# Twelve-sublayer decoder: a new order of the matmuls in the large experts, one indirect weight load per quad in the small experts

## Chip, cores and metric

One core of one Trainium2 chip runs the whole program. The metric is the device time of one execution in microseconds, as the median of several runs. Less is better.

## What is computed

The input `x` is 128 sequences of 64 tokens with 128 features (8192 tokens). Twelve sublayers follow one another, each `x = layernorm(x + f(x))`. They are attentions, feed-forward layers and mixtures of experts. The change touches three of them, the mixtures in which tokens are sorted by expert:

```python
# L0_attn ("moe_first"): 8 experts, top 2 of a softmax, 128 -> 512 -> 128, gelu
hid = gelu(x @ w1[e] + b1[e]); out = hid @ w2[e] + b2[e]; y = sum over the 2 chosen e of topw * out
# L1_ffn ("L_ffn" in the profile): 32 experts, top 1, 128 -> 32 -> 128, relu twice
h = relu(x @ w1[e] + b1[e]); y = relu(h @ w2[e] + b2[e])
# L3_ffn ("moe_last"): 8 experts, top 1 with a capacity, 128 -> 512 -> 128, gelu
```

All numbers are float32.

## The kernel before

Each of the three mixtures works in the same way. A router (matmuls and many small VectorE steps, `choose` and `plan`) gives every token a row, a "slot", in a buffer in HBM in which the tokens of one expert are contiguous. POOL scatters the token rows there (`slot_x`) with indirect DMAs, 128 rows each. The experts then run over tiles of slots, and POOL gathers the results back from `slot_y` with indirect DMAs, after which the residual sum and the layer norm are made. The tokens are cut into parts (16, 32 and 16 token tiles in the large mixtures, two halves in the small one), so that the scatters of the next part and the gathers of the part before are issued by POOL while the tiles of the present part run. POOL waits for counts of finished tiles (`out_done`) before some of its scatters, which spreads them over the tiles.

Large experts, `moe` (L665): `J` tiles of 256 slots, 85 in moe_first and 53 in moe_last. Every tile loads the packed weights of its expert (`load_expert` L970, 578 KB, one plain DMA from SP into one of `RING` = 4 buffers) and its rows (`load_slots` L981, 128 KB, one of `XRING` = 3). TensorE works in the order that the loop at L1074 to L1078 spells out: `hidden(j)` (L1048, the first matmuls, 4 of 256 columns into two PSUM banks), `turn(j + 1)` (L1039, two transposes of the next tile's rows), `output(j)` (L1059, the second matmuls, 8 of 128 columns, which need the gelu of tile j). The profile shows each float32 matmul as two instructions, so a tile has 8 at L1055 and 16 at L1066. ScalarE makes four gelus of a tile (L1113) and the copy of the next transposed rows (L1104). VectorE evicts the output with its bias (`evict` L931, L936). SP's queue runs, per tile, `load_slots(j + 3)`, `load_expert(j + 3)`, `store_slots(j)`; the store waits for the eviction of tile j, so the row load that stands behind it in the queue is issued after that eviction. There is one PSUM bank for transposes, and two for the hidden values, so `hidden(j + 1)` also waits for the gelus of tile j (L1051).

Small experts, `moe_small` (L2570): 32 "quads" of four slot tiles of 128, each slot tile with its own expert. `load_expert` (L2737) reads the expert's number into a register, then loads its first weights (16 KB, L2745) and its second ones with the biases (`down`, 32 KB, L2747); it runs four times per quad, for g = 0 and 2 on SP and for 1 and 3 on ScalarE's queue, three quads ahead. TensorE's order (L2853 to L2859) is already `turn(j + 2)`, `hidden(j + 1)`, `output(j)`. POOL's program (L2897 to L2925) issues the 32 scatters of part 0, then those of part 1, spread by waits for `out_done`, and then chunk after chunk four gathers and two small steps of the layer norm.

## Time and profile before

| | us |
|---|---|
| Median of 3 runs | 3681.12 (3676.68 to 3685.07) |
| The profiled execution, its own time | 3685.81 |
| Its span | 3684.1 |
| moe_first, first to last eviction of a tile | 103.0 to 579.1 (85 tiles) |
| Small experts, first to last eviction of a quad | 1708.1 to 1864.1 (32 quads) |
| moe_last, first to last eviction of a tile | 3397.5 to 3642.8 (53 tiles) |

PE is TensorE, DVE VectorE, ACT ScalarE, POOL GpSimd, SP SyncE; a "q" behind an engine's name is its queue of DMA issues and register work. In a timeline a row is a run of equal instructions, with its start, its duration from first start to last end, and in brackets how long the engine sat idle before it and what ended that. "remote" is an end of waiting that the profile can't put to a recorded instruction. PEclk is the granted clock of TensorE, 1.00 being 2.4 GHz and 0.50 being 1.2 GHz. A row by stretch has the stretch, its length, the busy time and number (x) of the instructions asked for, PEclk, the share of the DMA engines' time and GB/s.

### The profile page before, as it was taken

What the parts mean: (1) busy time and instruction counts of PE and PEld (TensorE: products, weight loads), DVE (VectorE), ACT (ScalarE), POOL (GpSimd) and SP (SyncE); (2) the same over time, 40 slices, a digit from 0 to 9 for tenths busy, and PEclk for the clock granted to TensorE, in tenths of its full rate; (3) what the DMA queues carried; (4) which work ended last, traced back from release to release, by engine and by line L of the source; (5) the groups of instructions that cost most, each with busy time, mean ns of one, the idle gap of its engine ahead of it and who ended that gap; (6) DMA issues with size and microseconds to landing.
All of it is one profiled execution on the core that took longest, in us unless ns stands there. A gap on an engine that the chain in (4) does not pass through costs nothing. (4 is left out here: it accounts for less than half of the span.)

```text
span 3684.1 us, 83888 instructions
## 1 busy us (share of the span) xinstructions
PE 2954.5 (80%) x28814; PEld 2049.7 (56%) x28814; DVE 2179.3 (59%) x5986; ACT 1819.7 (49%) x3516; POOL 1824.6 (50%) x1735
## 2 busy tenths in 40 slices
PE   2778877897888789953529997996999869995895
PEld 2667765674555556642316665664444536664784
DVE  2111134656888568862347886777898678884124
ACT  0333334744555456621216665775466676661342
POOL 3542254535777655526365554664033655553335
PEclk9988988899999799975559998998999889996997
DMA  8655652020101021214621112221000012222674
GB/s 283 185 168 177 187 163 86 24 8 25 41 35 45 38 72 69 71 45 119 171 59 43 58 54 88 83 89 54 1 1 1 2 29 64 73 66 87 198 218 145
DMA packets 325160, 315.45 MB, mean 86 GB/s; under 512 B 111348, under 2 KB 244885, under 8 KB 324504
## 3 DMA queue, kind: packets, MB, share of 16 engines
q1 hardware_dynamic: 283240, 261.98, 23.3%
q0 software_dynamic: 16384, 33.59, 3.0%
q10 hardware_dynamic: 25264, 16.40, 1.5%
q8 instruction: 154, 2.52, 0.3%
q14 instruction: 118, 0.97, 0.1%
HBM read 167.28 MB, written 60.69 MB: 62 GB/s over the span
## 5 line engine op out<-in xcount | busy, mean ns | idle before, releaser
L1066 PE MATMUL moe_first_out_ps<-moe_first_expert_w,moe_first_hid 128*128 128x128 f32 x1360 | 214.2, 310 | 92.5 <-ACT moe_first_hid L1113 55.1
L1113 ACT ACTIVATE moe_first_hid<-moe_first_hid_ps,moe_first_expert_w 128x256 f32<-128x256 f32 x340 | 139.2, 471 | 268.4 <-PE moe_first_hid_ps L1055 150.7
L936 DVE TENSOR_TENSOR moe_first_tile_y<-moe_first_out_ps,moe_first_expert_w 128x256 f32<-128x256 f32 x85 | 36.1, 425 | 379.2 <-PE moe_first_out_ps L1066 221.8
L1066 PEld LDWEIGHTS moe_first_out_ps<-moe_first_expert_w,moe_first_hid 128*128 128x128 f32 x1360 | 191.0, 211 | 110.3 <-DVE moe_first_tile_y L936 47.0
L1132 POOL DMA_INDIRECT slot_x<-x_tok,moe_first_slots x128 | 123.8, 968 | 109.6 <-DVE moe_first_slots L908 48.6
L1055 PE MATMUL moe_first_hid_ps<-moe_first_tile_xT,moe_first_expert_w 128*128 128x256 f32 x680 | 173.1, 400 | 3.1 <-issue 2.6
L794 POOL DMA_INDIRECT moe_first_token_y<-slot_y,moe_first_slots x128 | 123.8, 968 | 94.9 <-issue 66.7
L1865 POOL TENSOR_TENSOR causal_k_blocks<-causal_k_T,headmask 128x1024 f32<-128x1024 f32 x64 | 121.3, 1897 | 99.5 <-PE causal_scores L1475 94.0
L1865 POOL TENSOR_TENSOR alibi_k_blocks<-alibi_k_T,headmask 128x1024 f32<-128x1024 f32 x64 | 121.2, 1896 | 94.1 <-PE alibi_scores L1475 90.1
L1865 POOL TENSOR_TENSOR full_k_blocks<-full_k_T,headmask 128x1024 f32<-128x1024 f32 x64 | 120.7, 1896 | 84.2 <-PE full_scores L1475 79.2
L1113 ACT ACTIVATE moe_last_hid<-moe_last_hid_ps,moe_last_expert_w 128x256 f32<-128x256 f32 x212 | 86.6, 471 | 140.8 <-PE moe_last_hid_ps L1055 122.5
L3154 PE MATMUL L_ffn_experts<-weights_odd,x_T 128*128 128x512 f32 x256 | 146.5, 655 | 1.3 <-ACT L_ffn_expert_out L3250 1.3
L1865 POOL TENSOR_TENSOR keys_k_blocks<-keys_k_T,headmask 128x1024 f32<-128x1024 f32 x64 | 120.9, 1899 | 45.7 <-PE keys_scores L1475 42.1
L1055 PEld LDWEIGHTS moe_first_hid_ps<-moe_first_tile_xT,moe_first_expert_w 128*128 128x128 f32 x680 | 131.9, 205 | 20.6 <-issue 4.4
L1066 PE MATMUL moe_last_out_ps<-moe_last_expert_w,moe_last_hid 128*128 128x128 f32 x848 | 125.0, 295 | 21.6 <-issue 11.7
L3079 DVE SCALAR_TENSOR_TENSOR L_ffn_combined<-L_ffn_expert_out,L_ffn_mix,L_ffn_combined 128x128 f32<-128x128 f32 x448 | 128.7, 350 | 3.9
L1066 PEld LDWEIGHTS moe_last_out_ps<-moe_last_expert_w,moe_last_hid 128*128 128x128 f32 x848 | 110.5, 195 | 32.8 <-issue 16.0
L1865 POOL TENSOR_TENSOR diff_k_blocks<-diff_k_T,headmask 128x1024 f32<-128x1024 f32 x64 | 121.7, 1912 | 10.8 <-POOL diff_k_T L1852 5.9
L3315 POOL TENSOR_SCALAR L_ffn_ms_eps<-L_ffn_ms 128x4 f32<-128x4 f32 x16 | 3.7, 231 | 239.6 <-DVE L_ffn_ms L3087 239.4
L936 DVE TENSOR_TENSOR moe_last_tile_y<-moe_last_out_ps,moe_last_expert_w 128x256 f32<-128x256 f32 x53 | 22.4, 423 | 167.7 <-PE moe_last_out_ps L1066 125.5
L1722 DVE TENSOR_REDUCE keys_maxima<-keys_scores 128x8 f32<-128x512 f32 x128 | 87.7, 685 | 49.7 <-PE keys_scores L1475 48.7
L1619 ACT ACTIVATE diff_probs_T<-diff_pT 128x512 f32<-128x512 f32 x128 | 76.1, 595 | 79.5 <-PE diff_pT L1489 79.2
(561 smaller groups left out, 8941.3 us busy)
## 6 DMA issues: line engine op xcount, KB each, us to landing
moe_first_expert_w<-in_L_attn_experts SPq DMA_DIRECT2D x85, 578.0 KB
moe_last_expert_w<-in_L_ffn_experts SPq DMA_DIRECT2D x53, 578.0 KB
moe_first_tile_x<-slot_x SPq DMA_DIRECT2D x85, 128.0 KB
slot_y<-moe_first_tile_y SPq DMA_DIRECT2D x85, 128.0 KB
slot_x<-blank ACTq DMA_DIRECT2D x2, 4992.0 KB
L_ffn_tile_x<-slot_x SPq DMA_DIRECT2D x32, 256.0 KB
slot_y<-L_ffn_tile_y SPq DMA_DIRECT2D x32, 256.0 KB
moe_last_tile_x<-slot_x SPq DMA_DIRECT2D x53, 128.0 KB
```

The lines of the kernel that those rows point to most:

```text
L794: pool.indirect_dma_start(y_in[:, p, k, r, :], None, slot_y[part][0:NTS[part] * SLOT_TILE, :], bass.IndirectOffsetOnAxis(slots[:, part, r, ...
L936: dve.tensor_tensor(y_out[:, q, :, :], out_bank[q][:, 0:SLOT_TILE].rearrange("p (s d) -> p s d", s=SPAN), over(wall[:, j % RING, 2 * FF + ...
L1055: last = pe.matmul(hid_bank[h][:, SLOT_TILE * (b % 2):SLOT_TILE * (b % 2) + SLOT_TILE], wall[:, j % RING, 128 * b:128 * b + 128], xT[:, j ...
L1066: last = pe.matmul(out_bank[j % 2][:, D * s:D * s + D], hid[:, j % 2, b, TILE * s:TILE * s + TILE], wall[:, j % RING, FF + D * b:FF + D * ...
L1113: act.activation(hid[:, j % 2, b, :], hid_bank[b // 2][:, SLOT_TILE * (b % 2):SLOT_TILE * (b % 2) + SLOT_TILE], gelu, bias=wall[:, j % RIN ...
L1132: pool.indirect_dma_start(slot_x[part][:, :], bass.IndirectOffsetOnAxis(slots[:, part, r, t:t + 1], 0), net.x_tok[:, origin[part] + t, :], ...
L1619: act.activation(probs_T[:, t.p, 4 * g:4 * g + 4, :].rearrange("p k t -> p (k t)"), pT_bank[:, :], ACT.Copy)\
L1722: dve.tensor_reduce(maxima[:, t.p, heads], src, AX_X, ALU.max).then_inc(max_done, 1)
L1865: pool.tensor_tensor(k_blocks[:, t.p, :, :], keys.to_broadcast([128, 8, TILE]), lanes.to_broadcast([128, 8, TILE]), ALU.mult).then_inc(spr ...
L3079: last = dve.scalar_tensor_tensor(combined[:, p, k, :], expert_out[:, p, k, e, :], w, combined[:, p, k, :], ALU.mult, ALU.add)
L3154: pe.matmul(expert_bank[g][:, :], net.x_T[:, TILE * t:TILE * t + TILE], experts_s[:, 4 * g:4 * g + 4, :].rearrange("p e d -> p (e d)"), st ...
L3315: pool.tensor_scalar(ms_eps[:, :], ms[:, :], 1.0 / D, 1e-6, ALU.mult, ALU.add).then_inc(ms_eps_done, 1)
```

## The change

Large experts: TensorE's loop is now `turn(j + 2)`, `hidden(j + 1)`, `output(j)`, with `turn(0)`, `turn(1)` and `hidden(0)` ahead of it; ScalarE copies `copy_turned(j + 2)` after the gelus of tile j. The weight ring has five buffers, and SP loads weights four tiles ahead. The ring of rows still has three, loaded three tiles ahead.

Small experts: the four `down` loads of a quad from SP and ScalarE are replaced by one indirect DMA on POOL, which fetches 128 rows of 1028 bytes, 32 for each of the four experts. The row numbers are made by VectorE: five small steps once (`lane`), and six in each `plan`. POOL's program is one loop over the quads now: in step j the scatters of part 1 that are due, a chunk's gathers where one is due, `load_down(j + 3)`, and a layer norm step where one is due. TensorE waits for the two kinds of weights by two semaphores.

```diff
-    RING, XRING = 4, 3
+    RING, XRING = 5, 3
...
-                for j in range(3):
+                for j in range(4):
                     load_expert(j)
...
                     if j + 3 < J:
                         load_slots(j + 3)
-                        load_expert(j + 3)
+                    if j + 4 < J:
+                        load_expert(j + 4)
                     store_slots(j)
...
                 turn(0)
+                turn(1)
+                hidden(0)
                 for j in range(J):
-                    hidden(j)
+                    if j + 2 < J:
+                        turn(j + 2)
                     if j + 1 < J:
-                        turn(j + 1)
+                        hidden(j + 1)
                     output(j)
...
                 copy_turned(0)
+                copy_turned(1)
...
-                    if j + 1 < J:
-                        copy_turned(j + 1)
+                    if j + 2 < J:
+                        copy_turned(j + 2)
...
+                    for g in range(4):
+                        own = slice(H * g, H * g + H)
+                        last = dve.tensor_scalar(row_f[own, :], expert_f[own, :].rearrange("p (n g) -> p g n", g=4)[:, g, :],
+                                                 float(E - 1), float(H), ALU.min, ALU.mult)
+                    step(last)
+                    step(dve.tensor_tensor(row_at[:, :], row_f[:, :], lane[:, 0:1].to_broadcast([128, J]), ALU.add))
+                    dve.tensor_copy(down_at[:, part, :], row_at[:, :]).then_inc(planned, 1)
...
-                eng.dma_start(down[H * g:H * g + H, j % RING, :], w_down[bass.ds(e, 1), :, :].rearrange("o p w -> p (o w)"))\
...
-                    pe.wait_ge(w_landed[j % RING], 128 * (j // RING + 1))
+                    pe.wait_ge(w_landed[j % RING], 64 * (j // RING + 1))
+                    pe.wait_ge(d_landed[j % RING], 16 * (j // RING + 1))
...
+                def load_down(j):
+                    part, n = divmod(j, J)
+                    if j >= RING:
+                        pool.wait_ge(out_ready, j - RING + 1)
+                    if n == 0:
+                        pool.wait_ge(planned, 3 * part + 3)
+                    pool.indirect_dma_start(down[:, j % RING, :], None, rows,
+                                            bass.IndirectOffsetOnAxis(down_at[:, part, n:n + 1], 0)).then_inc(d_landed[j % RING], 16)
...
+                pool.wait_ge(planned, 1)
+                for t in range(K):
+                    scatter(0, t)
+                for j in range(3):
+                    load_down(j)
+                pool.wait_ge(planned, 4)
+                due = {}
+                for t in range(K):
+                    due.setdefault(1 + t * (J - 6) // K, []).append(t)
+                gather_at = {q - 2: c for q, c in after_quad.items()}
+                for j in range(ALL):
+                    if j in due:
+                        pool.wait_ge(out_done, j)
+                        for t in due[j]:
+                            scatter(1, t)
+                    if j in gather_at:
+                        gather(gather_at[j])
+                    if j + 3 < ALL:
+                        load_down(j + 3)
+                    if j - 1 in after_quad:
+                        tail.inverse_std(pool, after_quad[j - 1])
```

## Rows read from the trace of the kernel before

**Rows 1.** The page: share of TensorE, and the second matmuls of moe_first.
```profile
PE 2954.5 (80%) x28814; PEld 2049.7 (56%) x28814; DVE 2179.3 (59%) x5986; ACT 1819.7 (49%) x3516; POOL 1824.6 (50%) x1735
...
L1066 PE MATMUL moe_first_out_ps<-moe_first_expert_w,moe_first_hid 128*128 128x128 f32 x1360 | 214.2, 310 | 92.5 <-ACT moe_first_hid L1113 55.1
```

**Rows 2.** By stretch: busy us and number (x) of the evictions at L936.
```profile
195.00:223.00 28.00, 3.40 (x8) 1.00 0.75 223
223.00:286.00 63.00, 2.97 (x7) 0.76 0.46 136
...
3529.00:3575.00 46.00, 4.87 (x12) 1.00 0.77 232
```

**Rows 3.** Timeline (start, duration, engine, line, operation, count): TensorE over one steady tile.
```profile
337.08 1.89 PE L1055 MATMUL moe_first_hid_ps<-moe_first_tile_xT,moe_first_expert_w 128*128 128x256 f32 x8
...
339.03 1.36 PE L1066 MATMUL moe_first_out_ps<-moe_first_expert_w,moe_first_hid 128*128 128x128 f32 x8
...
340.23 1.06 PE L1066 MATMUL moe_first_out_ps<-moe_first_expert_w,moe_first_hid 128*128 128x128 f32 x8
...
341.12 1.89 PE L1055 MATMUL moe_first_hid_ps<-moe_first_tile_xT,moe_first_expert_w 128*128 128x256 f32 x8
```

**Rows 4.** Timeline: the eviction of the tile before, and the next row load.
```profile
337.28 0.42 DVE L936 TENSOR_TENSOR moe_first_tile_y<-moe_first_out_ps,moe_first_expert_w 128x256 f32<-128x256 f32 x1 [3.61 <-PE moe_first_out_ps L1066]
...
338.14 0.47 SPq L987 DMA_DIRECT2D moe_first_tile_x<-slot_x  x1
```

**Rows 5.** DMA issues: KB each, median us from issue to landing.
```profile
diff_xT_in<-x_T SPq DMA_DIRECT2D x16, 256.0 KB, 2.3
...
keys_x_in<-x_tok SPq DMA_DIRECT2D x16, 256.0 KB, 3.6
```

**Rows 6.** Timeline: moe_first while POOL issues sixteen indirect DMAs without a pause.
```profile
304.07 1.20 POOL L1132 DMA_INDIRECT slot_x<-x_tok,moe_first_slots  x1 [0.20 <-issue]
...
308.69 2.25 PE L1066 MATMUL moe_first_out_ps<-moe_first_expert_w,moe_first_hid 128*128 128x128 f32 x16
...
315.60 0.42 DVE L936 TENSOR_TENSOR moe_first_tile_y<-moe_first_out_ps,moe_first_expert_w 128x256 f32<-128x256 f32 x1 [8.66 <-remote]
...
323.19 0.94 POOL L794 DMA_INDIRECT moe_first_token_y<-slot_y,moe_first_slots  x1 [0.30 <-issue]
...
328.30 0.42 DVE L936 TENSOR_TENSOR moe_first_tile_y<-moe_first_out_ps,moe_first_expert_w 128x256 f32<-128x256 f32 x1 [12.27 <-PE moe_first_out_ps L1066]
```

**Rows 7.** By stretch: busy us and number of the evictions at L2708, small experts.
```profile
1708.00:1762.00 54.00, 7.61 (x11) 0.53 0.63 170
1762.00:1787.00 25.00, 4.16 (x6) 0.50 0.65 166
1787.00:1866.00 79.00, 10.27 (x15) 0.54 0.58 148
```

**Rows 8.** Timeline, SP's queue: a quad of the small experts, no indirect DMA.
```profile
1762.23 0.43 SPq L2767 DMA_DIRECT2D slot_y<-L_ffn_tile_y  x1
...
1765.53 0.34 SPq L2745 DMA_DIRECT2D L_ffn_expert_up<-in_L_ffn_up  x1
1766.08 0.33 SPq L2747 DMA_DIRECT2D L_ffn_expert_down<-in_L_ffn_down  x1
1766.46 0.43 SPq L2767 DMA_DIRECT2D slot_y<-L_ffn_tile_y  x1
```

**Rows 9.** Timeline of POOL and VectorE: small experts, three scatters to a quad.
```profile
1754.06 0.96 POOL L2905 DMA_INDIRECT slot_x<-x_tok,L_ffn_slots  x1 [0.30 <-issue]
...
1755.96 0.69 DVE L2708 COPY L_ffn_tile_y<-L_ffn_out_ps 128x512 f32<-128x512 f32 x1 [4.69 <-remote]
...
1756.92 0.96 POOL L2905 DMA_INDIRECT slot_x<-x_tok,L_ffn_slots  x1 [1.90 <-DVE L_ffn_tile_y L2708]
```

**Rows 10.** Timeline of POOL and VectorE: small experts, the first eight gathers.
```profile
1787.79 0.98 POOL L2917 DMA_INDIRECT L_ffn_token_y<-slot_y,L_ffn_slots  x1 [27.39 <-DMA slot_y<-L_ffn_tile_y]
...
1796.40 0.69 DVE L2708 COPY L_ffn_tile_y<-L_ffn_out_ps 128x512 f32<-128x512 f32 x1 [9.84 <-remote]
```

More of the change, by code:

```diff
@@ L2612, in moe_small @@
         expert_f, expert_of = sb("expert_f", [128, NT]), sb("expert_of", [128, PARTS, NT], I32)
+        below, lane_i, lane_of, lane = sb("below", [128, 1]), sb("lane_i", [128, 1], I32), sb("lane_of", [128, 1], I32), sb("lane", [128, 1])
+        row_f, row_at, down_at = sb("row_f", [128, J]), sb("row_at", [128, J]), sb("down_at", [128, PARTS, J], U32)
         up = sb("expert_up", [128, RING, 4, H])
@@ L2632, in moe_small @@
         scattered = [sem(f"rows_scattered{n}") for n in range(PARTS)]
-        w_landed = [sem(f"expert_landed{n}") for n in range(RING)]
+        w_landed = [sem(f"expert_up_landed{n}") for n in range(RING)]
+        d_landed = [sem(f"expert_down_landed{n}") for n in range(RING)]
         x_landed = [sem(f"slot_x_landed{n}") for n in range(XRING)]
@@ L2721, in _ @@
                 dve.wait_ge(fixed, 1)
+                step(dve.tensor_reduce(below[:, :], before[:, :], AX_X, ALU.add))
+                step(dve.tensor_scalar(lane_i[:, :], below[:, :], -1.0, None, ALU.add))
+                step(dve.tensor_scalar(lane_of[:, :], lane_i[:, :], H - 1, None, ALU.bitwise_and))
+                step(dve.tensor_copy(below[:, :], lane_of[:, :]))
+                step(dve.tensor_scalar(lane[:, :], below[:, :], -1.0, float(H - 1), ALU.mult, ALU.add))
                 for part in range(PARTS):
@@ L2742, in load_expert @@
                 if n == 0:
[L2743 removed]
+                    eng.wait_ge(planned, 3 * part + 2)
                 e = eng.value_load(expert_of[0:1, part, at:at + 1], min_val=0, max_val=E - 1)
                 eng.dma_start(up[:, j % RING, g, :], w_up[bass.ds(e, 1), :, :].rearrange("o p h -> p (o h)"))\
[L2746 to L2747 removed]
                     .then_inc(w_landed[j % RING], 16)
@@ L2899, in _, with scatter @@
                     pool.wait_ge(net.cleared[1 + n], 16)
-                for part in range(PARTS):
-                    pool.wait_ge(planned, 2 * part + 1)
-                    for t in range(K):
-                        if part and t:
-                            pool.wait_ge(out_done, J * (part - 1) + 1 + t * (J - 6) // K)
-                        pool.indirect_dma_start(slot_x[part][:, :], bass.IndirectOffsetOnAxis(slots[:, part, t:t + 1], 0),
-                                                net.x_tok[:, part * K + t, :], None).then_inc(scattered[part], 16)
+                def scatter(part, t):
+                    pool.indirect_dma_start(slot_x[part][:, :], bass.IndirectOffsetOnAxis(slots[:, part, t:t + 1], 0),
+                                            net.x_tok[:, part * K + t, :], None).then_inc(scattered[part], 16)
+                rows = w_down.rearrange("e p w -> (e p) w")
+                def load_down(j):
[6 more added lines that the diff above has]
+                                            bass.IndirectOffsetOnAxis(down_at[:, part, n:n + 1], 0)).then_inc(d_landed[j % RING], 16)
                 def gather(c):
@@ L2918, in gather @@
                                                 bass.IndirectOffsetOnAxis(slots[:, part, t:t + 1], 0)).then_inc(gathered[p], 16)
-                for c in range(CHUNKS):
-                    if c % PC == 0:
+                pool.wait_ge(planned, 1)
[19 more added lines that the diff above has]
+                        tail.inverse_std(pool, after_quad[j - 1])
+                for c in late:
+                    if c == late[0]:
                         gather(c)
-                    if (c + 1) % PC:
+                    if c + 1 < CHUNKS:
                         gather(c + 1)
```

2 lines of the change are left out of this document (removed).

## Prediction

> **What bounds the kernel now.** I read the page first: TensorE is busy for 80% of the span and no other engine for more than 59% [rows 1]. Only the three mixtures are touched, and they fill about 877 us between first and last eviction (476, 156 and 245 us in the table), so next I read how fast their tiles follow one another. In moe_first one tile follows another after 4.04 us where nothing disturbs (341.12 - 337.08) [rows 3], but 84 intervals take 476.1 us, 5.67 each, so 137 us go to something else. In moe_last 52 intervals take 245.3 us, 4.72 each, and 35 us are lost. The view by stretch shows where: 8 evictions fall into one stretch of 28 us, 7 into the next of 63 us [rows 2].
>
> In the steady tile TensorE has no gap, yet it isn't at its own pace. Its second matmuls come in two halves of eight. The last eight take 0.89 us (340.23 to 341.12), the first eight 1.20 us (339.03 to 340.23), for the same work [rows 3]. The first eight each need a gelu that ScalarE is only just making; the page lists that releaser for this line [rows 1]. That wait of 0.31 us per tile is what the new order can remove. The first matmuls and the two transposes fill the rest, 337.08 to 339.03.
>
> In the lost time nobody works: the second matmuls of a tile start at 308.69 and last 2.25 us, so they end at 310.94, but the eviction that needs them starts at 315.60 after 8.66 us of idle, ended "remote", and the one after it at 328.30. Through this stretch POOL issues sixteen indirect DMAs, 1.27 us apart (19.1 us over 15 intervals) [rows 6]. In the timeline every such stall of several us lies within a run of indirect DMAs and ends soon after it. I conclude that signals between engines pass badly while POOL issues them. This decides how I price the second half of the change, which gives POOL more of them.
>
> **Large experts: second matmuls one tile later.** In the steady tile the gelus of tile j now finish under output(j - 1), turn(j + 2) and the start of hidden(j + 1). The period becomes 4.04 - 0.31 = 3.73 us. Eight stretches with no run of indirect DMAs, or a short one, hold 51 evictions (the first and the last of them in rows 2), so up to 51 x 0.31 = 16 us.
>
> What is late next is the row load. turn(m) now stands straight behind output(m - 3); before, a whole tile's work more lay ahead of it. The load of rows m still leaves SP's queue behind the store of tile m - 4, that is after its eviction. From the end of output(m - 4) (337.08) to that issue (338.14) it is 1.06 us [rows 3, 4]. No row gives this load's own time to landing; loads of 256 KB take 2.3 to 3.6 us [rows 5]. From the landing to the end of output(m - 2) it is one full period, 3.73. Two periods are thus at least 1.06 + L + 3.73. With L = 2.3 this is 3.55 us per tile and doesn't bind; from L = 2.7 it binds; at L = 3.3 all the gain is gone; with L = 3.6 it is 4.20 us per tile, worse than now. A 128 KB load with little in front of it is nearest to 2.3, but DMA share is already 0.75 and 0.77 in such stretches [rows 2], so I let a tail of late loads take 0.1 us per tile: 51 x 0.2 = -10 us. turn is in order on TensorE, and hidden and output are queued behind it, so a late load costs its full lateness.
>
> In the disturbed tiles the order has a second effect. When signals stop, TensorE can run on through what is already released. Before, that ended at the second matmuls of the current tile, at most; now hidden(j + 1) and output(j) are both released by gelus of tile j, so up to hidden's and turn's 1.95 us (337.08 to 339.03) [rows 3] more gets done. But where this has used up the loaded rows, the restart waits for a store and a load (1.06 + 2.3 us), and the gain is gone. I count half of the 1.95 us, some 0.9 us at each restart. There are 24 runs of indirect DMAs behind the first scatter stretches of the two mixtures, like that in rows 6: -22 us. In the first scatter stretches themselves POOL sets the pace (64 scatters at 1.26 us are 81 us of 90), and I take 0. The fifth weight buffer and the load four tiles ahead keep the old lead in time: the wait for out_done before load_expert(j + 4) is the same as that before load_expert(j + 3) with four buffers. It costs and brings nothing, since the weights aren't what a steady tile waits for. Sum for the large experts: -32 us. Ends: -68 (0.31 on all 138 tiles and 25 on restarts) and +22 (138 x 0.16, rows always late).
>
> **Small experts: down weights from POOL.** Three stretches [rows 7].
>
> While part 1 is scattered, 11 evictions take 54 us. A run of three scatters ends at 1755.02, the eviction comes 0.94 us behind it, and POOL resumes 0.96 us after that [rows 9]. So a quad is the run (3.5 us) plus 1.9 us, 5.4 us, and this is what the stretch shows. One more indirect DMA makes the run 1.26 us longer, in ten quads: +12 us. Ends 0 (signals pass between the DMAs) and +13.
>
> Between scatters and gathers SP's queue sets the pace: store to store is 4.23 us without a gap. A down load costs from the end of the up issue (1765.87) to its own end (1766.41), 0.54 us, twice per quad on SP [rows 8]. Without both a quad could take 3.15 us. A lone indirect DMA now falls into each, so I take 0.6 us off in 6 quads: -4 us. Ends -6 and +7 (6 x 1.26).
>
> While gathers run, 15 quads take 79 us. Eight gathers in a row held one eviction back from the end of its matmuls to 1796.40, 9.84 us of idle [rows 10]. Here 13 loads come between 32 gathers; about 8 of them lengthen a run by 1.26 us: +10 us. Ends -13 (SP's relief of about 0.85 us counts in all 15 quads) and +16. load_down(j + 3) also queues behind four gathers (5 us) and their wait for stored tiles, and hidden(j + 3) waits for it; three quads of lead, 8 us and more, hide that.
>
> At the start four load_downs come behind the 32 scatters and before the first turns are signalled: +2 us, ends 0 and +5. The added VectorE steps (5 once, 6 in each plan, small) lie under the scatters of part 0, 32 x 1.26 = 40 us; uncovered they would be about 4 us. Sum: 12 - 4 + 10 + 2 = +20 us, ends -19 and +41.
>
> The Trainium skill, DMA: Bandwidth & Descriptors, section Rules for kernel authors, says to coalesce small transfers, as below 64 KB one pays mostly overhead; its section Anatomy of one DMA gives 2.0 us fixed for each DMA issued from GpSimd. By it four loads of 32 KB in one are a plain gain. The rows above agree only where SP's queue sets the pace [rows 8]; where POOL's runs do, the count on POOL is what costs [rows 9]. What that rule would make of the time is the first rival.
>
> **The sum.** -32 + 20 = -12 us. Against the profiled execution's own time, 3685.8, this is 3673.8; it lay 4.7 us above the median of the runs, so for the median 3681.1 - 12 = 3669 us.
>
> **Rivals.**
>
> First, the relief of the queues counts more than the runs on POOL: the small experts follow SP at about 0.5 us less per quad, 32 x 0.5 = -16 us, with -32 in the large ones: -48, 3633 us. For it: SP's queue is full in rows 8 and signals do pass at times within a run. Against: in two of three stretches the evictions follow the ends of the runs.
>
> Second, and slower: the rows land late. If a row load takes 3.6 us in most steady tiles, these cost 51 x 0.16 = +8 us, and every restart waits for rows, so nothing is gained there. With +20 in the small experts this is +28, 3709 us. It decides from L = 3.3 us on. For it: rows 5's upper end, and the shorter period makes the queues fuller. Against: the lower end, and that SP issues the rows right behind the store.
>
> Third, the two halves cancel: the restarts bring nothing beyond -10 to -20 and the small experts lose as much: about 3681 us. TensorE then waits for the same runs on POOL in another order.
>
> **How the numbers follow.** Forecast 0.42, first rival 0.20, second 0.22, third 0.16. A difference under 0.2% (7.4 us) can't be told from no change here. Faster by more: 0.20 from the first rival and 0.34 of the forecast, 0.54. Within: 0.08 of the forecast and 0.12 of the third, 0.20. Slower: 0.22 and 0.04, 0.26. The range reaches to both outer rivals, 3633 to 3706.
>
> **What would show it.** Steady tiles of moe_first every 3.7 to 3.8 us with both halves of L1066 equal (0.89 us); if they are 4.0 or more and TensorE's idle before L1044 is ended by the row load, the second rival is right. In the small experts 1.26 us more from eviction to eviction while part 1 is scattered; if they stay at 5.4 or fall, the first rival is. The prediction is wrong if the stalls aren't tied to POOL's runs, or if a load by row numbers costs POOL another time than a gather.

## The result, and the profile after

| | before, us | after, us |
|---|---|---|
| Median of 4 runs each, in turn on one chip | 3678.9 (3670.8 to 3685.1) | 3712.6 (3707.6 to 3715.8) |
| Span of the profiled execution | 3684.1 | 3713.8 |
| moe_first, first to last eviction | 476.1 | 465.6 |
| Small experts, first to last eviction | 156.0 | 183.7 |
| moe_last, first to last eviction | 245.2 | 246.4 |

The changed kernel takes 1.0089 times as long, 95% interval 1.0069 to 1.0109: 34 us more, where 12 us less was forecast. The stages say where. The small experts cost 28 us more (20 was forecast), and the large ones give back 9 us in sum instead of 32. A stretch that nobody touched, from the last eviction of the small experts to the first of moe_last, takes 1533.5 us before and 1540.8 after, and 1535.9 to 1541.8 us in the runs below with times like these. moe_first, with its stalls, varies by more: the new one takes 465.6 us here, and 475.6 and 458.8 us in two runs below. So I read single stages with care. One of the six executions of `small`, below, took 6130.7 us, and its ratio leaves that one out.

First the steady tile, in the timeline of the changed kernel: TensorE, VectorE's evictions, and SP's row load (start, duration, engine, line, operation).

```profile
378.94 0.42 DVE L936 TENSOR_TENSOR moe_first_tile_y<-moe_first_out_ps,moe_first_expert_w 128x256 f32<-128x256 f32 x1 [3.31 <-PE moe_first_out_ps L1067]
378.95 1.89 PE L1056 MATMUL moe_first_hid_ps<-moe_first_tile_xT,moe_first_expert_w 128*128 128x256 f32 x8
...
379.39 0.36 SPq L993 DMA_DIRECT2D slot_y<-moe_first_tile_y  x1
379.79 0.47 SPq L987 DMA_DIRECT2D moe_first_tile_x<-slot_x  x1
...
380.68 1.95 PE L1067 MATMUL moe_first_out_ps<-moe_first_expert_w,moe_first_hid 128*128 128x128 f32 x16
...
382.67 0.42 DVE L936 TENSOR_TENSOR moe_first_tile_y<-moe_first_out_ps,moe_first_expert_w 128x256 f32<-128x256 f32 x1 [3.31 <-PE moe_first_out_ps L1067]
...
383.20 0.44 PE L1045 MATMUL moe_first_turn_ps<-ident,moe_first_tile_x 128*128 128x128 f32 x2 [0.57 <-DMA moe_first_tile_x<-slot_x]
```

The sixteen second matmuls are one unbroken run now, where rows 3 had two uneven halves, and from eviction to eviction the tile takes 3.73 us (378.94 to 382.67), as worked out. But the transposes behind them wait: the load of the rows was issued at 379.79, and they were used at 383.20, 3.41 us later. The table of waits (engine and line, what it waited for: us in total, times, longest) has this for the whole of both mixtures:

```profile
PE moe_first_turn_ps L1045 <- DMA moe_first_tile_x<-slot_x: 46.5, 20, 8.3
PE moe_last_turn_ps L1045 <- DMA moe_last_tile_x<-slot_x: 32.8, 19, 3.8
PE moe_first_hid_ps L1056 <- ACT moe_first_hid L1118: 25.6, 13, 5.3
```

79 us of waiting for rows is what the second rival described. They are of two sorts. Each of these 39 waits can be paired with the eviction four tiles earlier, behind whose store the row load stands in SP's queue. For 12 of them (14 us) that eviction came at once behind its matmuls, and the load was slow, as above: 3.7 us from issue to use (median). For the other 27 (65 us) that eviction was itself held back, by 0.5 to 14 us, and the load was then as quick as the lower bound, 2.5 us (median). One of these 27:

```profile
353.37 1.95 PE L1067 MATMUL moe_first_out_ps<-moe_first_expert_w,moe_first_hid 128*128 128x128 f32 x16
...
357.10 1.95 PE L1067 MATMUL moe_first_out_ps<-moe_first_expert_w,moe_first_hid 128*128 128x128 f32 x16
358.99 0.76 DVE L936 TENSOR_TENSOR moe_first_tile_y<-moe_first_out_ps,moe_first_expert_w 128x256 f32<-128x256 f32 x2 [8.90 <-remote]
...
359.85 0.47 SPq L987 DMA_DIRECT2D moe_first_tile_x<-slot_x  x1
...
362.10 0.44 PE L1045 MATMUL moe_first_turn_ps<-ident,moe_first_tile_x 128*128 128x128 f32 x2 [3.05 <-DMA moe_first_tile_x<-slot_x]
```

The row of 358.99 holds two evictions at once: the first had been due behind the matmuls of 353.37, which end at 355.32. Only after it could the load be issued, and TensorE, which had run on meanwhile, waited 3.05 us for it. The third line of the table I had not expected at all: TensorE waits for ScalarE's gelus, the very wait that the new order was to remove, 13 times, 2 us on average.

The stretches of rows 2, by evictions again:

```profile
195.00:223.00 28.00, 2.55 (x6) 0.94 0.72 215
223.00:286.00 63.00, 3.99 (x10) 0.84 0.56 166
```

16 tiles pass in these 91 us, 15 before. The second stretch has 10 instead of 7, the first 6 instead of 8.

In the small experts POOL's run between two evictions is longer, as in this timeline of POOL and VectorE, which answers to rows 9:

```profile
1742.15 0.97 POOL L2920 DMA_INDIRECT slot_x<-x_tok,L_ffn_slots  x1 [2.71 <-DVE L_ffn_tile_y L2723]
1743.47 0.69 DVE L2723 COPY L_ffn_tile_y<-L_ffn_out_ps 128x512 f32<-128x512 f32 x1 [1.59 <-PE L_ffn_out_ps L2863]
...
1745.95 0.98 POOL L2931 DMA_INDIRECT L_ffn_expert_down<-in_L_ffn_down,L_ffn_down_at  x1 [0.30 <-issue]
1747.23 0.97 POOL L2920 DMA_INDIRECT slot_x<-x_tok,L_ffn_slots  x1 [0.30 <-issue]
...
1751.03 0.98 POOL L2931 DMA_INDIRECT L_ffn_expert_down<-in_L_ffn_down,L_ffn_down_at  x1 [0.31 <-issue]
...
1753.60 0.69 DVE L2723 COPY L_ffn_tile_y<-L_ffn_out_ps 128x512 f32<-128x512 f32 x1 [9.44 <-DMA moe_first_token_y<-slot_y,moe_first_slots]
...
1755.90 0.69 DVE L2723 COPY L_ffn_tile_y<-L_ffn_out_ps 128x512 f32<-128x512 f32 x1 [1.61 <-PE L_ffn_out_ps L2863]
```

Two quads' DMAs, eight in all, run without a pause from 1742.15 to 1752.01. One eviction still comes at their start (1743.47), the next only 1.59 us after their end, and then two come 2.3 us apart. (The gather of moe_first that the row of 1753.60 names as the end of VectorE's wait was done long before; what ended the wait isn't recorded.) Two quads in 12.4 us are 6.2 each, where rows 9 gave 5.4. Cut at the 12th and the 17th eviction, whose start times the timeline has, the small experts read:

| us between evictions | 1 to 12 (scatters) | 12 to 17 (quiet) | 17 to 32 (gathers) |
|---|---|---|---|
| before | 56.3 | 21.4 | 78.2 |
| after | 67.1 | 18.0 | 98.6 |

### The profile page after: what moved, and what is told of

Read it like the earlier page. It is cut to its first block and busy times, and to the rows that moved or that the text cites. A ratio compares the mean times of both kernels' runs of the same rounds, so it can differ in the third digit from the quotient of the medians.

```text
span 3713.8 us, 83586 instructions
## 1 busy us (share of the span) xinstructions
PE 2932.1 (79%) x28814; PEld 2039.1 (55%) x28814; DVE 2182.6 (59%) x6003; ACT 1829.6 (49%) x3516; POOL 1856.1 (50%) x1767
## 5 line engine op out<-in xcount | busy, mean ns | idle before, releaser
L936 DVE TENSOR_TENSOR moe_first_tile_y<-moe_first_out_ps,moe_first_expert_w 128x256 f32<-128x256 f32 x85 | 35.7, 423 | 373.2 <-PE moe_first_out_ps L1067 188.3
L1056 PE MATMUL moe_first_hid_ps<-moe_first_tile_xT,moe_first_expert_w 128*128 128x256 f32 x680 | 187.2, 423 | 41.7 <-ACT moe_first_hid L1118 25.6
L1067 PEld LDWEIGHTS moe_first_out_ps<-moe_first_expert_w,moe_first_hid 128*128 128x128 f32 x1360 | 177.9, 203 | 16.5 <-issue 9.9
L1067 PE MATMUL moe_first_out_ps<-moe_first_expert_w,moe_first_hid 128*128 128x128 f32 x1360 | 178.1, 285 | 9.7 <-issue 8.4
L1870 POOL TENSOR_TENSOR diff_k_blocks<-diff_k_T,headmask 128x1024 f32<-128x1024 f32 x64 | 121.7, 1913 | 10.9 <-POOL diff_k_T L1857 5.9
L936 DVE TENSOR_TENSOR moe_last_tile_y<-moe_last_out_ps,moe_last_expert_w 128x256 f32<-128x256 f32 x53 | 22.4, 424 | 177.7 <-PE moe_last_out_ps L1067 108.1
L1108 ACT ACTIVATE moe_first_tile_xT<-moe_first_turn_ps 128x256 f32<-128x256 f32 x85 | 32.9, 387 | 167.1 <-PE moe_first_turn_ps L1045 79.2
L1727 DVE TENSOR_REDUCE full_maxima<-full_scores 128x8 f32<-128x512 f32 x128 | 87.8, 686 | 45.8 <-PE full_scores L1480 44.8
L1727 DVE TENSOR_REDUCE causal_maxima<-causal_scores 128x8 f32<-128x512 f32 x128 | 87.8, 686 | 45.8 <-PE causal_scores L1480 44.8
```

The costliest lines, as they stand in the source:

```text
L936: dve.tensor_tensor(y_out[:, q, :, :], out_bank[q][:, 0:SLOT_TILE].rearrange("p (s d) -> p s d", s=SPAN), over(wall[:, j % RING, 2 * FF + ...
L1056: last = pe.matmul(hid_bank[h][:, SLOT_TILE * (b % 2):SLOT_TILE * (b % 2) + SLOT_TILE], wall[:, j % RING, 128 * b:128 * b + 128], xT[:, j ...
L1067: last = pe.matmul(out_bank[j % 2][:, D * s:D * s + D], hid[:, j % 2, b, TILE * s:TILE * s + TILE], wall[:, j % RING, FF + D * b:FF + D * ...
L1108: act.activation(xT[:, j % 2, :], turn_bank[:, 0:SLOT_TILE], ACT.Copy)\
L1727: dve.tensor_reduce(maxima[:, t.p, heads], src, AX_X, ALU.max).then_inc(max_done, 1)
L1870: pool.tensor_tensor(k_blocks[:, t.p, :, :], keys.to_broadcast([128, 8, TILE]), lanes.to_broadcast([128, 8, TILE]), ALU.mult).then_inc(spr ...
```

## The experiments

Each group below ran on one chip together with the kernel before, whose median there stands in the text. The groups fell on chips of two kinds, and this turned out to matter more than the change; the second group shows it.

**First group: the two halves, and a suspect in each.** Before: 3691.0 us. `large` and `small` are the two halves of the diff, each alone on the kernel before.

> The kernel before with the change of the two large mixtures alone: second matmuls behind the next tile's first ones, five weight buffers, expert loads four tiles ahead. The small experts are as before. The prediction's theory gives -32 us (10 from steady tiles, 22 from restarts behind POOL's runs). Its second rival, late rows, gives from the stages of the changed kernel -8 us in moe_first and +3 us in moe_last: -5 us. TensorE's idle before the transposes of the rows, ended by the row load, was 46.5 us in moe_first and 32.8 us in moe_last of the changed kernel; it should be there again if the second rival is right.

> The kernel before with the change of the small experts alone: down weights of a quad by one indirect load from POOL. The prediction gives +20 us; the stage of the changed kernel reads +27 us (first to last eviction 183.7 us against 156.0). If the two halves of the change are independent, large and small together are what the whole change cost, 34 us (3712.6 against 3678.9); if not, the rest of it, some 7 us in stages that were not touched, belongs to neither.

`large` measured 3691.6 us, ratio 1.0002 (0.9991 to 1.0012); `small` 3717.4 us, 1.0067 (1.0048 to 1.0086), +25 us. So the small experts make nearly the whole loss, and the large ones bring nothing. Together this is 25 us of the 34; the intervals leave room for the rest. In the result's own two traces 7 us of it lie in the untouched stretch named above. In `small` the three stretches are 67.9, 18.0 and 98.5 us, as in the changed kernel.

`large_x4` gives the new order a fourth row buffer:

```diff
-    RING, XRING = 5, 3
+    RING, XRING = 5, 4
...
-                    if j + 3 < J:
-                        load_slots(j + 3)
                     if j + 4 < J:
+                        load_slots(j + 4)
                         load_expert(j + 4)
```

> As large, with a fourth row buffer and the rows loaded four tiles ahead instead of three, so that each row load leaves SP's queue one store earlier. If late rows ate the gain (second rival), most of the 46.5 + 32.8 us of waits for row loads go, steady tiles take 3.73 us, and the time falls to between 30 and 60 us below before. If the row load only stood last among waits that POOL's runs prolong anyway, it stays within 8 us of large.

It measured 3664.1 us, 0.9931 (0.9916 to 0.9946): 27 us faster than `large` and than before, 3 us short of the 30 to 60 that were expected if late rows ate the gain, and far from the 8 us of the other theory. TensorE's waits for rows in `large`:

```profile
PE moe_first_turn_ps L1045 <- DMA moe_first_tile_x<-slot_x: 45.8, 23, 8.9
PE moe_last_turn_ps L1045 <- DMA moe_last_tile_x<-slot_x: 30.2, 19, 3.7
```

In the same table of `large_x4` the transposes wait for no rows in moe_first, but for the copy that empties their bank, and the gelus stand first:

```profile
PE moe_first_hid_ps L1055 <- ACT moe_first_hid L1117: 39.3, 19, 5.8
...
PE moe_first_turn_ps L1044 <- ACT moe_first_tile_xT L1107: 13.0, 7, 5.1
```

In moe_last 5.1 us of row waits are left of 30.2, by the list of instruction groups (busy us, mean ns | idle before them, what ended it):

```profile
L1044 PE MATMUL moe_last_turn_ps<-ident,moe_last_tile_x 128*128 128x128 f32 x106 | 21.3, 284 | 8.0 <-DMA moe_last_tile_x<-slot_x 5.1 <-ACT moe_last_tile_xT L1107 3.0
```

Of 76 us of waiting for rows 27 us turned into time. The rest went to other waits; the table lists those for gelus and for the copy, and I haven't traced each.

`small_std` moves the layer norm's inverse deviation ahead of the turn's loads on POOL:

```diff
+                    if j - 1 in after_quad:
+                        tail.inverse_std(pool, after_quad[j - 1])
                     if j in due:
...
-                    if j - 1 in after_quad:
-                        tail.inverse_std(pool, after_quad[j - 1])
```

> As small, but on POOL the layer norm's inverse deviation of a chunk comes ahead of the scatters, gathers and the down load of the same turn instead of behind them. Theory A: TensorE's transposes, SP's stores of finished rows and VectorE's normalise wait in order for that small operation, and the new place behind four gathers and a load cost part of the 27 us; then this is 8 to 15 us faster than small. Theory B: the number of indirect DMAs on POOL is all that counts; then it is within 3 us of small.

It measured 3712.0 us, 1.0062 (1.0046 to 1.0078), 5 us less than `small` by the medians, 2 by the ratios. Neither theory is hit; alone, this move returns little.

**Second group: rows alone, and POOL's program alone.** Before: 3503.2 us on this chip.

> The kernel before once more, for the stage times on the chip on which the three runs beside it run. Stages that nobody touched are expected within 5 us of the profile of before: the large and large_x4 runs showed them 3 to 6 us longer or shorter.

> The kernel before with a fourth row buffer and the row load four tiles ahead, and nothing else: the old order of the second matmuls and four weight buffers. Theory A: in the old order no row is late, the fourth buffer is worth something only to the new order, and this is within 4 us of before. Theory B: the fourth row buffer by itself gives the 27 us by which large_x4 is faster than large; then this is 20 us or more faster than before.

> The kernel before with POOL's program in the small experts rewritten turn by turn as in the changed kernel, but with no down load on POOL: the eight plain down loads of a quad stay on the queues of SP and ScalarE. If the 27 us of the small experts come from the indirect loads themselves, this is within 4 us of before; if they come from the new order of scatters, gathers and inverse deviations on POOL, it is 15 us or more slower.

> As small, but the indirect down load goes to a spare buffer, and the eight plain loads of before still bring the weights that are used. Against small it shows what the queues of SP and ScalarE gain from having no down loads; against small_loop, what one more indirect DMA per quad costs. The prediction has 24 us for the DMAs on POOL and 4 us back for SP's relief, so by it this is 4 us slower than small; by its first rival (the relief is worth 0.5 us in each of 32 quads) it is 16 us slower than small.

`rows_x4` measured 3502.5 us, 1.0000 (0.9985 to 1.0015). A fourth row buffer is worth nothing to the old order here; it pays only where the new order needs the rows early. On a chip with stalls this pair was not run. There the trace of before speaks for it: its transposes wait for rows in no tile of moe_first or moe_last, and from issue to use of the rows it is 9.3 and 8.8 us (medians of the two mixtures), against 3.0 and 3.2 in the changed kernel and 6.8 and 6.4 in `large_x4`.

`small_loop`, with no down load on POOL at all, measured 3516.3 us, 1.0037 (1.0024 to 1.0049), +13 us: the rewritten order of POOL's program costs by itself, nearly the 15 us that were expected if it is to blame. `small_twice` measured 3530.6 us, 1.0081 (1.0053 to 1.0109), 14 us above `small_loop`: that is one indirect DMA per quad. Whether it is 4 or 16 us slower than `small` can't be read, since `small` was not run on this chip. Its stretches are 54.1, 21.3 and 91.5 us against 46.3, 21.9 and 82.9 in `small_loop`. The quiet stretch tells of SP's relief: with the plain loads still on SP it stays at 21.3, without them (`small`) it is 18.0, against 21.4 before. Relief is worth 3.4 us there; for the other two stretches no pair of runs on one kind of chip isolates it.

`base` is the kernel before, and measured 3503.7 us (1.0007, 0.9994 to 1.0021). Its trace shows what the chip does otherwise. The second stretch of rows 2 by evictions:

```profile
223.00:286.00 63.00, 6.76 (x16) 1.00 0.79 236
```

and POOL and VectorE in a run of sixteen indirect DMAs:

```profile
211.33 0.96 POOL L1132 DMA_INDIRECT slot_x<-x_tok,moe_first_slots  x1 [0.30 <-issue]
212.01 0.42 DVE L936 TENSOR_TENSOR moe_first_tile_y<-moe_first_out_ps,moe_first_expert_w 128x256 f32<-128x256 f32 x1 [3.62 <-PE moe_first_out_ps L1066]
212.59 0.99 POOL L794 DMA_INDIRECT moe_first_token_y<-slot_y,moe_first_slots  x1 [0.30 <-issue]
...
216.05 0.42 DVE L936 TENSOR_TENSOR moe_first_tile_y<-moe_first_out_ps,moe_first_expert_w 128x256 f32<-128x256 f32 x1 [3.61 <-PE moe_first_out_ps L1066]
```

16 evictions instead of 7, every 4.04 us, straight through the run of POOL that holds one back by 8.66 and 12.27 us in rows 6. POOL's own DMAs take the same 0.96 us, 1.26 us apart. moe_first takes 360.0 us instead of 476.1. On this chip evictions aren't held back. In all, the kernel before takes 3679 to 3691 us on three chips (that of the result among them) and 3501 to 3503 us on three others; the traces from the former have the stalls, those from the latter don't.

**Third group: the same on a chip with stalls.** Before: 3680.4 us.

> The kernel of large again. On one chip the kernel before takes 3503 us instead of 3679 to 3691, moe_first ends 135 us earlier there, and its evictions follow one another every 4.04 us straight through POOL's scatters. If this run is on such a chip, nothing stalls, the 0.31 us of the gelu wait can count in nearly all 138 tiles (-43 us), and late rows take some of it: 15 to 40 us faster than before is expected. If it is on a chip like the first ones, 0 as there.

> The kernel of large_x4 again. On a chip without stalls: up to 138 x 0.31 = 43 us faster than before, and faster than large_b by what late rows cost there (5 to 25 us). On a chip with stalls: 27 us faster than before, as in large_x4.

> The kernel of small_loop again. On the chip without stalls it was 13 us slower than before. On a chip with stalls it tells how the 26 us of small divide: 13 us again if an inverse deviation behind four gathers costs its lateness whatever the chip; near 0 if the indirect loads make all of the 26 us there.

> The kernel of small_std again. On a chip without stalls the order of the inverse deviations should matter more and the count of indirect DMAs less: if the 13 us of small_loop are the two inverse deviations that stand behind gathers, this is at most 13 us slower than before. On a chip with stalls: 21 to 23 us slower, as in small_std.

The chip was of the kind with stalls. `large_b`: 3677.5 us, 0.9995 (0.9983 to 1.0007). `large_x4_b`: 3648.0 us, 0.9907 (0.9884 to 0.9930), 30 us below `large_b` and 32 below before, where 27 was expected. `small_loop_b`: 3697.6 us, 1.0046 (1.0030 to 1.0062), +17 us. `small_std_b`: 3701.4 us, 1.0057 (1.0039 to 1.0076), +21 us. The transposes of the layer norm on TensorE while gathers run (x28: busy us, mean ns | idle before them, what ended it), in before, `small_loop_b` and `small_std_b`:

```profile
L638 PE MATMUL L_ffn_xT_ps<-ident,x_tok 128*128 128x128 f32 x28 | 7.8, 434 | 20.8 <-issue 17.1 <-DVE x_tok L627 3.8
```

```profile
L638 PE MATMUL L_ffn_xT_ps<-ident,x_tok 128*128 128x128 f32 x28 | 7.8, 434 | 38.7 <-DVE x_tok L627 36.2 <-issue 2.6
```

```profile
L638 PE MATMUL L_ffn_xT_ps<-ident,x_tok 128*128 128x128 f32 x28 | 7.8, 435 | 26.0 <-issue 19.4 <-DVE x_tok L627 6.6
```

In POOL's new program four of the eight inverse deviations stand behind four gathers of a later chunk, 5 us; VectorE's normalise waits for it, TensorE's transposes wait in order for that (36.2 us instead of 3.8), and hidden and output are queued behind them. `small_std_b` heals this wait (6.6), and yet the gather stretch stays at 94.6 us, against 91.8 in `small_loop_b` and 78.2 before (76.9 to 79.2 in `large`, `large_x4` and their repeats, whose small experts are the old ones). With the order healed, the 13 loads in this stretch cost 16.4 us, which is what 13 x 1.26 gives. In this stretch each fault alone costs 14 to 16 us and both together 20 (98.6 against 78.2): they hide each other in part.

**Fourth group: what is left.** Before: 3501.3 us, a chip without stalls. `loop_std` is `small_loop` with the move of `small_std`. `x4_four_w` is `large_x4` with four weight buffers. `few` gathers one of four token tiles of a chunk in the large mixtures.

> As small_loop (no down load on POOL), but each inverse deviation ahead of the scatters and gathers of its turn. On POOL the gathers and inverse deviations then follow one another as in the kernel before. If the 13 to 17 us of small_loop are the inverse deviations that stood behind four gathers, this is within 4 us of before. If they come from where the gathers themselves now lie, it stays 10 us or more slower.

> As large_x4, but with four weight buffers as before, and each expert's weights loaded three tiles ahead. The prediction says that the fifth buffer only keeps the old lead in time, so that without it the lead is one tile shorter. If weights have room, this equals large_x4 within 5 us; if they have none, TensorE's idle before the first matmuls is ended by the weight load and this is 10 us or more slower than large_x4.

> The kernel before, but in the two large mixtures only one of a chunk's four token tiles is gathered and its rows are used for all four: 96 indirect DMAs fewer in moe_first, 48 in moe_last (the result is left wrong by that). Theory A: TensorE's stalls come from POOL's runs of indirect DMAs, some 0.6 us for each DMA (162 us lost for 256 of them in moe_first); on a chip with stalls moe_first's 476 us between first and last eviction fall by about 60 us, moe_last's 245 us by 15 to 30. Theory B: they have another cause; then only the end of each mixture is shorter, by a few us.

> large_x4 with the same gathers left out. If the new order with four row buffers is worth 0.31 us in each undisturbed tile and nothing at a restart, its gain against few grows with the number of undisturbed tiles: from the 27 to 34 us that it has with all gathers to 30 to 43 us (138 x 0.31). If its gain came mostly from restarts, it falls with the number of runs, below 20 us.

`loop_std`: 3502.4 us, 1.0004 (0.9993 to 1.0015), and the gather stretch is 71.0 us against 71.2 in `base`. So the 13 us of the rewritten program on such a chip are the place of the inverse deviations. That the 17 us on a chip with stalls are the same is likely from the waits above, but `loop_std` was not run there.

`x4_four_w`: 3512.0 us, 1.0027 (1.0017 to 1.0036), 11 us slower than before. `large_x4` was not run on such a chip, so this is no price of the fifth buffer. The loss stands in moe_first, 370.2 us against 360.0 in `base`; moe_last takes 214.6 against 215.8, though TensorE waits there for weights 10 times, against once, for 1.6 us, in `base` (us in total, times, longest):

```profile
PE moe_last_hid_ps L1056 <- DMA moe_last_expert_w<-in_L_ffn_experts: 10.6, 10, 3.3
```

`few`: 3450.6 us, 0.9848 (0.9827 to 0.9868). Fewer gathers help here as well, but moe_first only goes from 360.0 (`base`, another chip without stalls) to 344.6 us; whether they take the stalls away could not be seen, as this chip had none. `few_x4`: 3437.3 us, 0.9818 (0.9796 to 0.9840), 13 us below `few`, where 30 to 43 was expected. The stages: moe_last 210.2 to 195.0 us, 15.2 of the 16 that 52 x 0.31 gives; moe_first 344.6 to 342.7 us, 2 of 26. In moe_first 11 intervals take 5.69 us. ScalarE and TensorE in one of them, in `few_x4`:

```profile
301.61 0.38 ACT L1109 ACTIVATE moe_first_tile_xT<-moe_first_turn_ps 128x256 f32<-128x256 f32 x1 [1.16 <-PE moe_first_turn_ps L1046]
305.56 0.60 ACT L645 ACTIVATE x_T<-moe_first_route_ps 128x512 f32<-128x512 f32 x1 [3.57 <-PE moe_first_route_ps L638]
306.05 1.57 ACT L1119 ACTIVATE moe_first_hid<-moe_first_hid_ps,moe_first_expert_w 128x256 f32<-128x256 f32 x4
...
301.41 1.89 PE L1057 MATMUL moe_first_hid_ps<-moe_first_tile_xT,moe_first_expert_w 128*128 128x256 f32 x8
303.14 1.95 PE L1068 MATMUL moe_first_out_ps<-moe_first_expert_w,moe_first_hid 128*128 128x128 f32 x16
304.92 0.60 PE L638 MATMUL moe_first_route_ps<-ident,x_tok 128*128 128x128 f32 x4
...
307.03 1.97 PE L1057 MATMUL moe_first_hid_ps<-moe_first_tile_xT,moe_first_expert_w 128*128 128x256 f32 x8 [1.29 <-ACT moe_first_hid L1119]
```

The first matmuls of tile j + 1 end at 303.30. ScalarE could start their gelus, but in its queue `copy_transposed` of the layer norm stands ahead (L645), and that waits for the transposes (L638), which TensorE does only behind `output(j)`. The gelus start at 306.05, and TensorE stands still for 1.29 us before the next first matmuls. Before the change no gelu stood behind such a copy, since the first matmuls of tile j + 1 came behind the layer norm's transposes anyway.

**Fifth group: that queue mended.** Before: 3502.4 us, again a chip without stalls.

```diff
+                    if j - 3 in after_tile:
+                        tail.copy_transposed(act, after_tile[j - 3], route_bank)
                     if j + 2 < J:
                         copy_turned(j + 2)
-                    if j - 2 in after_tile:
-                        tail.copy_transposed(act, after_tile[j - 2], route_bank)
...
+                if J - 3 in after_tile:
+                    tail.copy_transposed(act, after_tile[J - 3], route_bank)
```

> As large_x4, but on ScalarE the copy of the transposed layer-norm rows comes behind the next tile's four gelus instead of ahead of them. few to few_x4 gained 15 us in moe_last (52 x 0.31 = 16) and only 2 us in moe_first, where 12 intervals take 5.69 us instead of 3.73: in each the gelus of tile j + 1, whose first matmuls are long done, stand in ScalarE's queue behind a copy that waits for output(j) and the layer norm's transposes. If that is it, this is 12 x 1.96 = 24 us faster than large_x4 where nothing stalls (some 35 to 45 us faster than before), and 10 to 24 us faster on a chip with stalls (40 to 50 us faster than before). If the 5.69 us have another cause, it equals large_x4 within 4 us.

> As large (three row buffers, rows three tiles ahead), with the same move on ScalarE. It separates the two faults of the new order: if each costs for itself, this is 10 to 24 us faster than large, and x4_gelu_first is faster still by the 27 to 31 us that the fourth row buffer was worth on chips with stalls. If late rows take what the gelus give back, it is within 5 us of large.

`x4_gelu_first`: 3482.8 us, 0.9943 (0.9926 to 0.9961), 20 us faster than before and the fastest whole kernel on these chips. `large_gelu_first`, with three row buffers: 3513.9 us, 1.0031 (1.0020 to 1.0042), 11 us slower than before; between the two, the fourth row buffer is worth 31 us here, as on the chips with stalls (27 and 30). Neither `large` nor `large_x4` was run on a chip without stalls, so what the move on ScalarE alone is worth in time, expected at 10 to 24 us, no pair of runs shows. `large_gelu_first` shows late rows without any stall: apart from the first tile of each mixture, TensorE waits for them 47 times, 40 us, and in 45 of these waits the eviction four tiles earlier had come at once; the load was slow. In this run and in `x4_four_w` the trace has landings of part of the row loads (KB each, median us from issue to landing), first `large_gelu_first`, then `x4_four_w`:

```profile
moe_first_tile_x<-slot_x SPq DMA_DIRECT2D x85, 128.0 KB, 3.4
...
moe_last_tile_x<-slot_x SPq DMA_DIRECT2D x53, 128.0 KB, 2.6
```

```profile
moe_first_tile_x<-slot_x SPq DMA_DIRECT2D x85, 128.0 KB, 3.1
...
moe_last_tile_x<-slot_x SPq DMA_DIRECT2D x53, 128.0 KB, 3.4
```

ScalarE in `x4_gelu_first`, in a tile with the layer norm's copy:

```profile
269.50 0.38 ACT L1107 ACTIVATE moe_first_tile_xT<-moe_first_turn_ps 128x256 f32<-128x256 f32 x1 [1.16 <-PE moe_first_turn_ps L1044]
270.43 1.64 ACT L1117 ACTIVATE moe_first_hid<-moe_first_hid_ps,moe_first_expert_w 128x256 f32<-128x256 f32 x4 [0.54 <-PE moe_first_hid_ps L1055]
273.45 0.60 ACT L645 ACTIVATE x_T<-moe_first_route_ps 128x512 f32<-128x512 f32 x1 [1.38 <-PE moe_first_route_ps L638]
```

The gelus go ahead, and such an interval takes 4.17 us instead of 5.69, 1.5 us less, in 5 of 12 cases; in most of the others something else is late too. moe_first is 351.3 us against 360.0 in `base` and 370.2 in `x4_four_w`, which lacks both the move and the fifth weight buffer. The expected 35 to 45 us against before were missed. 138 x 0.31 is 43. One part of what is missing stands in the trace, at the first tile of moe_first's second part:

```profile
167.81 0.36 SPq L987 DMA_DIRECT2D moe_first_tile_x<-slot_x  x1
...
170.00 0.69 PE L1044 MATMUL moe_first_turn_ps<-ident,moe_first_tile_x 128*128 128x128 f32 x2 [5.14 <-DMA moe_first_tile_x<-slot_x]
```

These rows can be loaded only when POOL has scattered them all (167.8 us; 167.4 in `base`). `base` used them at 174.3, the new order wants them at 164.9: this eviction comes 11.98 us behind the one before, 8 us late. Another part is that TensorE waits 18.9 us for the layer norm's rows in moe_first, against 10.9 in `base`. For the rest I have no measured split. `x4_gelu_first` was not run on a chip with stalls.

## Why the prediction was wrong

**The steady tile: right.** 4.04 became 3.73 us, the halves are equal, and where nothing else interferes (moe_last, `few` to `few_x4`) 15.2 of 16 us came.

**The price of late rows: this step failed, in two places.** The first is "I let a tail of late loads take 0.1 us per tile". The condition was written down (from L = 3.3 us on the gain is gone), the bounds 2.3 and 3.6 us lay on either side of it, and I took the lower as nearer. The loads measured later take 2.6 to 3.4 us (medians), and 3.41 us lie between issue and use in the steady tile above. The second is "I count half of the 1.95 us" at a restart. The sum said itself that a restart which has used up its rows waits for a store and a load and gains nothing, and then still counted 22 us for 24 restarts. On the chip with stalls this is the larger place: 27 of the 39 waits for rows, 65 of 79 us, follow an eviction that was held back, and there even a load at the lower bound came too late. In time, late rows cost 27, 30 and 31 us in three comparisons that changed nothing else (`large_x4` to `large`, twice, and the pair of the fifth group), against 5 us (51 x 0.1) and half of each restart in the sum. The second rival was right here, and its 3709 us lies nearest to the 3712.6 measured, though it got there by +8 in the large experts where 0 was measured.

**"24 restarts x 0.9 = -22" with rows on time: open.** Of the 38 us that the sum had before late rows took their part in steady tiles (16 + 22), four row buffers brought 27 and 32. moe_last on chips with stalls falls to 226.5 and 227.5 us from 242.3 to 245.2. That is what 52 x 0.31 gives, but the forecast had given moe_last only 20 steady tiles, 6 us, so some 10 us came in disturbed tiles, and whether per tile or per restart can't be told. In moe_first the gelus behind ScalarE's copy come on top, and no run separates them on such a chip. I had asked what is late next for TensorE and for SP, and did not go through ScalarE's queue: `hidden(j + 1)` now comes ahead of the layer norm's transposes, but its gelus still stood behind the copy that waits for them.

**The fifth weight buffer at nothing: open.** The only run without it, `x4_four_w`, had weights late in moe_last and takes 9 us more there than `x4_gelu_first` (214.6 against 205.3), but the two differ in the move on ScalarE as well and ran on different chips.

**Small experts: right in mechanism, short in size.** While part 1 is scattered, +12 was forecast, and +10.8 came (56.3 to 67.1 us). Quiet quads, -4: -3.4. The start, +2: the changed kernel's first eviction comes 12.2 us after the last scatter of part 0, 12.1 before: 0. The gathers, +10: +20.4. There the step that failed is "about 8 of them lengthen a run": with the order healed the stretch grew by 16.4 us, as if all 13 did. On top comes what I had not looked at, that the loop which carries the new loads also moves the inverse deviations behind gathers (14 us by itself, 3 to 4 beside the loads). The Trainium skill, DMA: Bandwidth & Descriptors, section Rules for kernel authors, says to coalesce small transfers; the runs disagree for this kernel: the loads in one cost 14 us on POOL even where its DMAs stall nobody (`small_twice` against `small_loop`), and the relief of the other queues is worth 3.4 us.

**The sum.** The large experts at 0 instead of -32 are most of the 46 us between -12 and +34, the small ones at +25 to +28 instead of +20 another 5 to 8. The rest, some 8 us, was in neither half when run alone. In the traces 7 us stand in the stretch between the small experts and moe_last, which the change didn't touch, and why is open. The range ended at 3706 us, short of the second rival's own 3709; no case in it had both halves worse than their likeliest value.

## What to carry to other kernels

When an order is changed on one engine, go through the queue of every engine that serves it and ask, for each in-order wait, whether what stands behind it is now needed earlier: rows on SP cost 27 to 31 us here, and an inverse deviation behind gathers on POOL 13 to 17; gelus behind a copy on ScalarE cost 1.5 us in the undisturbed tiles with a layer norm chunk. A load that is used a stage earlier needs a buffer more, and that buffer is worth nothing before (0, on a chip without stalls) and the whole gain after (27 to 31 us). When a bound decides between gain and loss and the rows lie on both sides of it, the loss deserves more than a tail.

## What the runs showed of the hardware

The same kernel takes 3679 to 3691 us on some chips and 3501 to 3503 us on others, 5% apart, and on each chip its runs lie within 0.4% of their median. Most of the difference is in the stalls of rows 6: on one kind, work on other engines whose inputs are done often starts late while POOL issues indirect DMAs back to back; on the other it starts at once, at the same 0.96 us and 1.26 us spacing of these DMAs. moe_first alone is 116 us shorter there (476.1 to 360.0). That signals are what is held back is my reading; the traces show only the late starts. Nor do they all last as long as the run: in rows 6 the first stall ends at 315.60, 8.5 us before the sixteenth DMA is done (324.13). `few`, which would have changed the number of DMAs, fell on a chip without stalls. What makes a chip the one or the other no run here shows. I had taken the stalls for a property of the design, and half of my sum rested on them. POOL's order in the small experts costs nearly the same on both kinds (13 and 17 us), and the fourth row buffer as well (31; 27 and 30).

A 128 KB row load took 2.6 to 3.4 us from issue to landing while weights streamed (medians of the two mixtures in `large_gelu_first` and `x4_four_w`, on chips without stalls), where loads of 256 KB elsewhere took 2.3 to 3.6 us [rows 5].

A load by row numbers costs POOL about what a gather does: 0.98 us, and the next DMA starts 1.28 us after it (1745.95 to 1747.23).
